# Token-layout halves and DMA transposes from the third block on, in a fused attention and feed-forward kernel

## The reference

```python
xn = layernorm(x)                                # over the 256 channels, no gain, no bias
h = tanh(xn @ W1.T + b1); s = h @ w2.T + b2      # one score per token
e = exp(s - max(s)); num = cumsum(e * xn); den = cumsum(e)    # along the 4096 tokens
attn = tanh(concat(num / den, xn) @ Wc.T + bc)
gate, up = xn @ wg.T, xn @ wu.T                  # int weights / 127, 256 -> 768
ffn = (silu(gate) * up) @ wd.T                   # 768 -> 256
out = x + attn + ffn
```

## Time and profile before

| | |
|---|---|
| three runs | 417.21, 415.43, 417.17 us; median 417.17 us |
| profiled execution | 415.07 us, of which the span (first to last instruction) is 413.3 us |
| mean granted TensorE clock | 0.996 of full |
| busy | PE 402.4, DVE 311.8, ACT 251.1, POOL 165.0 us |
| transposes on PE (L571) | 128 matmuls |
| DMA | 29.50 MB, 24431 packets |

### The profile page before, as it was taken

How to read it: one execution, slowest core, us unless ns; L and a number is a source line. 1 busy time by engine, 2 the same in 40 slices (tenths; PEclk the granted TensorE clock), 3 DMA queues, 4 the chain that set the end, 5 groups by cost and what they waited for, 6 DMA issues and landing times.

```text
span 413.3 us, 7888 instructions
## 1 busy us (share of the span) xinstructions
PE 402.4 (97%) x2857; PEld 282.2 (68%) x2857; DVE 311.8 (75%) x664; ACT 251.1 (61%) x465; POOL 165.0 (40%) x228
## 2 busy tenths in 40 slices
PE   8779999999999999999999999999999999999996
PEld 3436767676758768667868677686766677686765
DVE  5698999999789998778685866788667578655351
ACT  3888586858498684873883855536445453536350
POOL 0250220131306996728070520788618367402000
PEclk9899999999999999999999999999999999999999
DMA  8997000000003252131100011422221220101001
GB/s 257 338 349 227 2 3 0 2 1 2 0 19 90 51 142 67 50 78 43 61 27 25 28 51 32 127 74 80 103 76 50 79 87 16 52 2 52 27 26 59
DMA packets 24431, 29.50 MB, mean 71 GB/s; under 512 B 1216, under 2 KB 19648, under 8 KB 24384
## 3 DMA queue, kind: packets, MB, share of 16 engines
q1 hardware_dynamic: 24384, 28.91, 22.9%
HBM read 20.45 MB, written 8.45 MB: 70 GB/s over the span
## 4 chain that ended last, share of the span: by engine, by line
PE 69%; DVE 18%; issue 5%; SPq 2%; DMA 2%; ACT 2%; POOL 2%; DVEq 0%; ACTq 0%; POOLq 0%
PE bank L578 32%; PE bank L603 29%; PE bank L623 7%; DVE stats L791 3%; DVE bank L928 3%; DVE ex L951 2%; DVE wide L933 2%; DMA tri<-in_tri 2%; DVE bank L913 2%; PE bank L571 1%; DVE xres L937 1%; DVE xt L903 1%; DVE mv L795 1%; SPq L1097 1%; POOL wide L1039 1%
## 5 line engine op out<-in xcount | busy, mean ns | idle before, releaser
L603 PE MATMUL bank<-xt,narrow 128*128 128x512 f16 x768 | 179.7, 381 | 0.9 <-DVE xt L903 0.7
L603 PEld LDWEIGHTS bank<-xt,narrow 128*128 128x128 f16 x768 | 75.1, 98 | 76.7 <-issue 1.7
L578 PE MATMUL bank<-narrow,wide 128*128 128x256 f16 x792 | 96.3, 273 | 0.0
L578 PE MATMUL bank<-narrow,xt 128*128 128x256 f16 x768 | 92.9, 274 | 3.0 <-ACT bank L698 3.0
L578 PEld LDWEIGHTS bank<-narrow,xt 128*128 128x128 f16 x768 | 75.2, 98 | 19.5 <-issue 3.4
L578 PEld LDWEIGHTS bank<-narrow,wide 128*128 128x128 f16 x792 | 77.5, 98 | 9.4
L729 ACT ACTIVATE sg<-bank 128x512 f32<-128x512 f32 x96 | 57.3, 597 | 40.4 <-PE bank L603 40.2
L736 ACT ACTIVATE wide<-bank 128x512 f16<-128x512 f32 x90 | 53.8, 598 | 44.1 <-DVE bank L928 43.4
L928 DVE SCALAR_TENSOR_TENSOR bank<-bank,sg 128x512 f32<-128x512 f32 x96 | 66.3, 695 | 16.7 <-PE bank L603 16.0
L1039 POOL TENSOR_TENSOR wide<-ex,wide 128x512 f16<-128x512 f32 x32 | 39.2, 1243 | 92.5 <-ACT wide L749 92.5
L933 DVE TENSOR_TENSOR wide<-bank,wide 128x512 f16<-128x512 f32 x90 | 60.7, 678 | 16.8 <-ACT wide L736 16.0
(11 more groups left out here) (82 smaller groups left out, 274.8 us busy)
## 6 DMA issues: line engine op xcount, KB each, us to landing
rows<-scratch SPq DMA_DIRECT2D x16, 512.0 KB, 4.8
out_y<-xres SPq DMA_DIRECT2D x32, 256.0 KB, 2.1
xres<-in_x SPq DMA_DIRECT2D x15, 512.0 KB, 8.9
wide<-in_wg SPq DMA_DIRECT2D x1, 768.0 KB, 6.6
wide<-in_wu SPq DMA_DIRECT2D x1, 768.0 KB, 7.9
wide<-in_wd SPq DMA_DIRECT2D x1, 768.0 KB, 10.5
xres<-in_x SPq DMA_DIRECT2D x2, 256.0 KB, 3.1
wide<-in_wc SPq DMA_DIRECT2D x1, 512.0 KB, 9.4
```

What stands on the lines that cost most here:

```text
L578: return pe.matmul(dst, lhs, rhs, start=False, stop=stop, skip_group_check=True)
L603: mm = pe.matmul(b[:, :], pg.up(which, k, j), pg.xn(sx, k, tok), start=n == 0, stop=n == len(todo) - 1)
```

## The change

1. For blocks 2 to 15 (`FIRST_T = 2`) the narrow program has no `Lb` and no `Xl`. `Xh` (ACT) makes the high half straight from `xnat`, in token layout. The new step `Xm` (POOL) makes the low half, `xnat` minus high. Both go to a waiting place in `xt` itself: the columns of block 15 while i < 14, of block 0 from then on (`waiting`). The new step `Tx` (SP) issues two DMA transposes per half, each of [128 tokens, 512 f16] into the four 128x128 squares (s, k) of `xt16`. Each of the four tiles of a block has a semaphore of its own.
2. `Xh` of a block waits until the transposes of the block before have landed (the waiting place is free), `Ln` waits for the `Xm` of the block before, and `S`, `Gg`, `Gu`, `C` and `N` for the landed transposes. The scale 1024 goes into rstd and shift in the last Newton step.
3. x of blocks 3 to 15 is loaded by steps `Lx` in SP's order, each before the block's `B`. The Newton iteration on POOL is three steps in place of one.
4. The opening: w1 and ident are issued before wg, x of block 1 before wd, x of block 2 before wc; the two bias rows, w2b2 and tri are issued by ACT, with semaphores of their own; `Sv` waits for w2b2 alone. `Wgh` on ACT comes after the second `Xh` of block 0, `Kg` after `Wgh`. 22 warm-up matmuls in place of 25; `Ss` waits for the last.
5. The places: `Lb` and `S` at 2.5 + 3.55 (i - 1); some entries of `STEP` are different.

The core of the diff:

```diff
@@ due times
-            due["Xh", i, pr], due["Xl", i, pr] = end["Lb", i, pr] + 0.1, end["Lb", i, pr] + 0.8
+            if i >= FIRST_T:
+                due["Ln", i, pr] = due["S", i, pr] - 8.7
+                due["Tx", i, pr], due["Xm", i, pr] = due["S", i, pr] - 5.5, due["S", i, pr] - 7.0
+            due["Xh", i, pr] = due["S", i, pr] - 7.6 if i >= FIRST_T else end["Lb", i, pr] + 0.1
@@ STEP
-    "T": (PO, 4.0, 4.1), "N": (PO, 2.5, 2.6), "Cl": (PO, 1.2, 1.3),
+    "T": (PO, 1.35, 1.45), "N": (PO, 2.8, 2.9), "Cl": (PO, 1.2, 1.3), "Xm": (PO, 1.2, 1.3),
+    "Lx": (SY, 0.6, 4.0), "Tx": (SY, 1.0, 4.0),
@@ needs
+    if kind == "Xh" and turned[0] == "Tx":
+        return [(("Ln", i, x), 0), *([(("Tx", i - 1, x), 0)] if i > FIRST_T else []),
+                *([(("C", 0, 1), 0)] if i == SPARE_TO else [])]
+    if kind == "Xm":
+        return [(("Xh", i, x), 0), *([(("Xm", i, 0), 0)] if x else [])]
+    if kind == "Tx":
+        return [(("Xm", i, x), 0), *([(("Tx", i, 0), 3.5)] if x else []), *([(("Tx", LAST - 1, 1), 0)] if i == LAST else [])]
@@ helpers
+        def waiting(i, pr):
+            b = LAST if i < SPARE_TO else 0
+            return xt16[:, pr, :, b * BLK:(b + 1) * BLK]
...
             def x_ready(self, i, pr):
-                return (a_x, self.nth("Xh", i, pr)) if self.wide else (v_xlo, self.nth("Xl", i, pr))
+                if self.wide:
+                    return [(a_x, self.nth("Xh", i, pr))]
+                if i < FIRST_T:
+                    return [(v_xlo, self.nth("Xl", i, pr))]
+                return [(s_t[t], 16 * (i - FIRST_T + 1)) for t in (2 * pr, 2 * pr + 1)]
@@ ACT
+            elif kind == "Xh" and i >= FIRST_T and not pg.wide:
+                act.wait_ge(a_xn, pg.nth("Ln", i, n))
+                if i == SPARE_TO:
+                    act.wait_ge(p_y, pg.nth("C", 0, 1))
+                elif i > FIRST_T:
+                    for s, count in pg.x_ready(i - 1, n):
+                        act.wait_ge(s, count)
+                act.activation(waiting(i, n)[:, :, 0:D], xnat[:, n, :, :], ACT.Copy).then_inc(a_x, 1)
@@ POOL
+            elif kind == "Xm":
+                pool.wait_ge(a_x, pg.nth("Xh", i, k))
+                pool.tensor_tensor(waiting(i, k)[:, :, D:], xnat[:, k, :, :], waiting(i, k)[:, :, 0:D],
+                                   ALU.subtract).then_inc(g_xm, 1)
@@ SP
+            if kind == "Lx" and i >= FIRST_X:
+                load_x(sp, i)
+            elif kind == "Tx":
+                sp.wait_ge(g_xm, pg.nth("Xm", i, n))
+                if (i, n) == (LAST, 0):
+                    for t in range(4):
+                        sp.wait_ge(s_t[t], 16 * (LAST - FIRST_T))
+                for t in (2 * n, 2 * n + 1):
+                    lo = i * BLK + t * P
+                    sp.dma_start_transpose(xt16[:, :, :, lo:lo + P].rearrange("p s k t -> p (s k) t"),
+                                           waiting(i, n)[:, t % 2, :]).then_inc(s_t[t], 16)
@@ opening, SP
+            sp.dma_start(w1_32, halves(w1)).then_inc(s_w1, 16)
+            sp.dma_start(ident[:, :], ident_in).then_inc(s_ident, 16)
             sp.dma_start(half(wg32.bitcast(I32)), halves(wg)).then_inc(s_wg, 16)
-            sp.dma_start(ident[:, :], ident_in).then_inc(s_ident, 16)
-            sp.dma_start(w1_32, halves(w1)).then_inc(s_w1, 16)
             sp.dma_start(half(wu32.bitcast(I32)), halves(wu)).then_inc(s_wu, 16)
-            sp.dma_start(bias[:, :], biases.partition_broadcast(P)).then_inc(s_bias, 16)
+            load_x(sp, 1)
+            sp.dma_start(wd32.bitcast(I32).rearrange("p (k n) -> p k n", k=KH), halves(wd)).then_inc(s_wd, 16)
+            load_x(sp, 2)
             sp.dma_start(wc_32, halves(wc)).then_inc(s_wc, 16)
-            sp.dma_start(wd32.bitcast(I32).rearrange("p (k n) -> p k n", k=KH), halves(wd)).then_inc(s_wd, 16)
-            sp.dma_start(w2b2[:, :], w2b2_in.partition_broadcast(P)).then_inc(s_cst, 16)
-            load_x(1)
-            sp.dma_start(tri[:, :], tri_in).then_inc(s_cst, 16)
-            for i in range(2, NBLK):
-                load_x(i)
```

More of the change, by code:

```diff
@@ L37 @@
 BANKS = 8
+NEWTON = 3
 SG_RING = 3
@@ L141, in due_times @@
         if g:
-            first = due["Lb", blocks[0], 0]
+            first = due["S", blocks[0], 0] - (6.5 if blocks[0] >= FIRST_T else 2.0)
             for n, i in enumerate(blocks):
-                due["B", i, 0], due["B", i, 1] = first - 13.0 + 2.0 * n, first - 12.0 + 2.0 * n
-            due["R", g, 0], due["T", g, 0] = first - 8.5, first - 8.4
+                due["B", i, 0], due["B", i, 1] = first - 10.0 + 2.0 * n, first - 9.0 + 2.0 * n
+                if i >= FIRST_X:
+                    due["Lx", i, 0] = first - 18.0 + 2.0 * n
+            due["R", g, 0] = first - 8.5
+            for n in range(NEWTON):
+                due["T", g, n] = first - 8.4 + 1.4 * n
     for i in range(NBLK):
@@ L268, in needs, with may_precede @@
     return [((chain[kind], i, x), 0)] if kind in chain else []
+def may_precede(st):
+    kind, i, _ = st
+    return kind in WEIGHTS + ONCE or (kind in AHEAD and i < (1 if kind in ("Hh", "Hl", "D") else 2))
 class Plan:
@@ L284, in __init__ @@
         self.open_now, self.freed = set(), dict.fromkeys(range(BANKS), 0.0)
-        self.done = {st: (SY, 0.0) for st in once}
+        self.done = {st: (SY, 0.0) for st in [*once, *(st for st in DUE if wide and st[0] in WEIGHTS)]}
         self.free = dict(BEGIN)
-        skip = {*self.done, *([] if wide else [("Ln", 0, 0), ("Ln", 0, 1)])}
+        skip = {*self.done, *(st for st in DUE if not (st[0] not in WEIGHTS + ("Xm", "Tx") if wide else
+                                                       st[1] < FIRST_T if st[0] in ("Lb", "Xl") else
+                                                       st[1] >= FIRST_T if st[0] in ("Xm", "Tx") else
+                                                       st[:2] != ("Ln", 0)))}
         self.todo = {e: sorted((st for st in DUE if STEP[st[0]][0] == e and st not in skip), key=DUE.get)
@@ L290, in __init__ @@
         self.order = []
-        self.times = {0.0, *BEGIN.values(), *SENT.values(), *(15.0 + 1.6 * i for i in range(NBLK))}
+        self.times = {0.0, *BEGIN.values(), *SENT.values(), 9.2, 9.9, 13.4, 17.2}
         while any(self.todo.values()):
@@ L313, in ready @@
     def ready(self, e, st):
[L314 to L317, removed]
+        t = (0, 13.4, 17.2)[st[1]] if st[0] == "B" and st[1] < FIRST_X else SENT.get(st[0], 0.0)
+        if not self.wide and (BRANCH_OF[e], 0, 0) not in self.done and not may_precede(st):
             return None
@@ L584, in scores @@
                 pe.wait_ge(a_ss, pg.nth("Ss", i, pr))
-                pe.wait_ge(*pg.x_ready(i, pr))
+                for s, count in pg.x_ready(i, pr):
+                    pe.wait_ge(s, count)
                 for t in range(2):
@@ L597, in hidden @@
                 if j == 0:
-                    pe.wait_ge(*pg.x_ready(i, 1))
+                    for s, count in [*pg.x_ready(i, 0), *pg.x_ready(i, 1)]:
+                        pe.wait_ge(s, count)
                 if i == 0 and not pg.wide:
@@ L777, in scalar_program @@
                 act.wait_ge(p_d, pg.plan.earlier["D"])
-                act.activation(wg32, wg32.bitcast(I32), ACT.Copy, scale=INV127).then_inc(a_w, 1)
+                act.wait_ge(g_xm, pg.plan.earlier["Xm"])
+                for st in EARLY:
+                    if st[0] == "Tx":
+                        for s, count in fits.x_ready(*st[1:]):
+                            act.wait_ge(s, count)
+                act.activation(wg32, wg32.bitcast(I32), ACT.Copy, scale=INV127).then_inc(a_32, 1)
             for kind, i, n in pg.plan.late(SE):
@@ L813, in root_seed, with root_newton @@
             step(dve.tensor_scalar(rstd[:, t].bitcast(I32), seed[:, t], -1.0, MAGIC, ALU.mult, ALU.add))
-        def root_newton(eng, s, g, done):
+        def root_newton(eng, s, g, done, its):
             t, n = columns(g), [done]
@@ L823, in root_newton @@
             eng.wait_ge(v_rs, SEED_STEPS * (g + 1))
-            for _ in range(NEWTON):
+            for it in its:
                 step(eng.tensor_tensor(newton[:, t], rstd[:, t], rstd[:, t], ALU.mult))
@@ L830, in root_newton @@
                     continue
-                step(eng.tensor_scalar(newton[:, t], newton[:, t], 1.0, 1.5, ALU.mult, ALU.add))
+                up = X_UP if it == NEWTON - 1 else 1.0
+                step(eng.tensor_scalar(newton[:, t], newton[:, t], up, 1.5 * up, ALU.mult, ALU.add))
                 step(eng.tensor_tensor(rstd[:, t], rstd[:, t], newton[:, t], ALU.mult))
-            if g:
+            if g and NEWTON - 1 in its:
                 step(eng.tensor_tensor(shift[:, t], mv[:, t, 0], rstd[:, t], ALU.mult))
```

124 lines of the change are left out of this document (75 added, 49 removed).

## The result

The changed kernel takes 413.17 us (median of 20 runs, 410.2 to 416.13), the kernel before 416.5 (20 runs, 415.43 to 419.06): ratio 0.9912, interval 0.9889 to 0.9934. It is faster by 0.9%. I had said 402.5 with a range from 397.5 to 412.0. The sign was right; the size was off by 10.7 us, and the time lies outside the range. The profiled execution took 412.01 us, span 410.1.

A forecast was written before the change was run, and what follows sets the result against it. TensorE was taken as the bound from 30 us on. From 415.07 us, transposes -12.3, opening -2.5, POOL +0.5 and DMA stalls +1.0 gave 401.8, stated as a median of 402.5 us, range 397.5 to 412.

The forecast's parts named there:

- What bounds the kernel: From 30 us on, TensorE's own work sets the span; what leaves its queue leaves the time.
- The sum: Whole kernel: 415.07 - 12.3 - 2.5 + 0.5 + 1.0 = 401.8 us, stated as a median of 402.5.
- The transposes, 12.3 us: TensorE, blocks 2 to 15: 112 transposes leave at 0.11 us each, all 12.3 us counting as gain.
- VectorE: Low halves go, 19.1 us less work, no direct gain; busy under 19 of 20 us in 70 to 90.
- SP and the DMAs: SP's queue: DMA transposes cause no stall when issued on time; 1.0 us added for Tx behind O, bounds 0 and 14.
- the middle: Landing time of a half's DMA transposes: 4.0 us from packets, between a 2.1 us lower and 12 us upper bound.
- landing later than the order assumes: Rival, chance 0.11: halves land after 6 to 7 us, S stalls once a block, 12.6 us given back, about 415.
- the serial rival: Rival, chance 0.06: DMA squares don't overlap, 12 us a half, the waiting-place loop binds the score phase, about 470 us.
- POOL, 0.5 us: GpSimd: Xm's 34.8 us hidden on average, 0.5 us cost around 127 to 158 us, bounds 0 and 5.0.
- The opening, 2.5 us: Start of kernel: first S 1.4 us sooner, near 12.1; with clock and DVE wait 2.5 us gained, bounds 0 and 4.4.
- The clock: Opening: 1.7 us lost at the 1.2 GHz level after TensorE's idle time; half, 0.8 us, counted as gained.

The follow-up runs named there:

- e4: Changed kernel without Ln, Xh, Xm and Tx for blocks 2 to 15, whose readers take block 1's transposed x: 405.26 us, ratio 0.9723.
- e8: Changed kernel with Xm moved from GpSimd to VectorE, and Xh of block 14 also waiting for block 13's transposes: 412.89 us, ratio 0.9914.
- e3: Changed kernel without the DMA transposes; Ln, Xh, Xm still run, and readers of blocks 2 to 15 take block 1's transposed x: 408.04 us, ratio 0.9796.
- e9: Changed kernel with the STEP entry for Tx at the measured price (2.6, 5.2) in place of (1.0, 4.0): 406.55 us, ratio 0.9741.
- the table of doses: Changed kernel with Tx's believed seen time varied: 2.6 gave 417.55 us, 4.0 (unaltered) 413.17, 4.6 408.31, 5.2 406.55, 6.5 407.90; queue time varied too.
- e10: Changed kernel with Ln, Xh, Xm and Tx due 4.0 us sooner, the price of Tx left at (1.0, 4.0): 408.59 us, ratio 0.9802.
- e5: Changed kernel with two waiting places in turn, so Xh waits for the transposes of the block before the last: 414.64 us, ratio 0.9932.
- e1: Changed kernel with FIRST_T = NBLK: no DMA transposes; the new opening, x loads in steps, three-part Newton and new places remain: 414.52 us, ratio 0.9952.
- the ladder: Medians of the kernels with successive omissions: e1 414.52 us, e4 405.26, e3 408.04, the changed kernel 413.17.

## Why the prediction was wrong, step by step

- **What bounds the kernel: right.** TensorE from 30 us on. e4 shows it: with nothing in its way TensorE is idle for 2.0 us between 30 and 400. (The sum has a slip at its end: 401.8 us and the 2.1 between the profiled execution and the median make 403.9, not 402.5. Inside the range it changes nothing.)
- **The transposes, 12.3 us: right in kind, 9.3 us in medians,** 11.2 for one execution of each at equal clock, 12.9 by the estimate from mean clocks. No run holds the clock fixed. The 390 ns a transpose of the Trainium skill ("VectorE: DVE Perf Modes", section "The three transpose paths") would be 43.7 us by an estimate; the runs are far from it.
- **VectorE:** the low halves went as said (their group fell from 21.5 to 2.7 us of busy time), and I priced no wait on it. It set one: the 2.2 us at 117, at `V1` behind statistics. In 70 to 90 it was busy for 19.52 us, not under 19. As a whole its load was no bound: e8 gives it the low halves back and the time is the same, though GpSimd's relief is in that too.
- **SP and the DMAs: this is the step that failed.** I wrote "I take the middle, the estimate made from most rows: no stall when issued on time", so a late landing was priced at nothing. The 1.0 us that I added was for a `Tx` held behind an `O`; the trace has that from 168.5 to 170.6, and no `S` waited for it. The half takes 5.0 us, not 4.0; `S` waited 0.60 and 1.80 us for landings at 47 and 60, before the first output. Without the transfers the time is 5.1 us lower (e3), with an order that allows for them 6.6 (e9). My estimate priced the bytes and not the queue. By the page the queue's share grew from 22.9% of 413.3 us to 33.3% of 410.1: 41.9 us of all 16 engines, 1.5 us a half where I had 4.0. The rest is two issues of 1.27 us and the latency of 2.5, which no packet count shows. That I came near the true 5.0 was luck; that the order had been made with 4.0 I read, and then used my own 4.0 to call it safe. The bounds of this term were 0 and 14 us, the range of the whole reached to 412: the range left out the high end of the term.
- **The rival "landing later than the order assumes" was the right one,** at a chance of 0.11. I had it decide from 6.5 us a half, since `Tx` is due 5.5 us ahead of `S`. A due time only sorts the steps that are ready; what keeps `S` behind `Tx` in the order is the seen time of 4.0. So a landing later than 4.0 is enough, as the table of doses bears out (earlier due times also help, 4.6 us in e10, since a step that is ready is then taken sooner). Nor did `S` stall once a block, as I had it: of 6.8 us more idle time between 30 and 400, 2.4 are `S` waiting for a landing, twice in all; 2.2 are `V1` on VectorE and 2.0 late seeds of `S`, 1.8 of them behind `Ln`, which waits for `Xm`. I had named ScalarE's queue and called its wait for the waiting place free. It was not free of waiting, 8.0 us, but in the changed kernel no stall of TensorE over 0.3 us is shown to come from it; in e5 one of 2.5 us does. ("VectorE: DVE Perf Modes", section "The three transpose paths" of the Trainium skill, gives 1309 ns for a 128x128 square by DMA. Four of these one after another would be 5.2 us by an estimate; the trace has 2.5 us for the four of one transfer, so that the serial rival is out.)
- **POOL, 0.5 us: too little.** The conversions cost 2.8 us (e3 against e4), inside the bounds of 0 and 5.0. `Xm` takes 1197 ns as priced (1243); the stall that the traces show is `Ln` behind it at 167 to 171, where GpSimd has hardly a gap, 1.8 us in the changed kernel and in e3. The 2.8 us are those of `Ln` and `Xh` as well, and moving `Xm` away (e8) gained nothing.
- **The opening, 2.5 us: 2.0 measured, by another way.** The first `S` came later, not sooner, so the size came right by luck. That x of block 1 and w1 are issued sooner and that `Sv` doesn't wait for tri are possible reasons, as are the new places and Newton's three steps; none was run by itself.
- **The clock.** I counted half of one fall as a gain. The profile of the changed kernel has one more fall than that of the kernel before, and its runs are spread with their mean clock: 0.996 goes with 410.2 and 410.8 us, 0.985 with 413.98, 414.67 and 415.07, 0.979 with 416.13. The fall between 30 and 50 isn't shown to be the transfers' doing: e4 and e9, where `S` waits for no landing, show 0.91 there too, and e5, where it does, shows 1.00.

The measured parts add up to 416.5 - 2.0 (e1) - 9.3 (e4) + 2.8 + 5.1 = 413.1, against 413.17. They must, since each is the step from one rung of the ladder to the next; the sum is no further evidence.

What stays open: what turns 2.4 us of waits at `S` into 4.6 to 6.6 us of the median (e10, e9), and why two waiting places, which took away most of ScalarE's waits, gave nothing at all (e5). Its profile shows a late seed behind an `Xh` that waits for a landing, and the clock at 0.91 in 170 to 190, but no run isolates these.

## What to carry to other kernels

Where the order of the queues is fixed by a table of durations, a new kind of transfer is first a new entry: time it by issue on the queue and by landing, not by bytes, and set the entry at or a little above. Here too low cost several times the error (an entry 1.0 us under the measured time cost 6.6 us), too high cost nothing that could be told from the best. And when work is moved off the engine that bounds, look first for the waits that end on that engine: a total of waits on another engine (8.0 us on ScalarE) says little until one of them is followed to a stall, and the largest stall of the changed kernel past the opening ended with a softmax step that the change had left as it was.

## What the runs showed of the hardware

- A DMA transpose of [128, 512] f16 within SBUF holds SP's queue for 1.27 us (median of 56) and lands 2.5 us after that, at most 5.7; a plain store of 256 KB lands after 2.2.
- Beside four small transfers issued by ScalarE at the start, two loads of 256 KB that SP issued at the same time landed after 5.8 us. With the four held back (e2) it was 3.0, in the kernel before 3.1.
- Eight float32 transposes of 128x128 take TensorE 0.88 us by their starts, 0.11 us each. The kernel without 112 of them (e4) gives 9.3 us in medians, 0.08 each, and 11.2 at equal clock, 0.10.
